# A Mamba cross-attention block with a folded feed-forward: softplus in one ScalarE operation, the dt·u product on VectorE

## The chip, the cores and the metric

The kernel runs on one core of a Trainium2 chip. A core has TensorE (matmuls, into PSUM), VectorE, ScalarE (table-driven functions), GpSimd (which reads and writes SBUF only here) and SyncE, which issues most of the DMAs. Engines run their own instruction streams and wait for each other on semaphores. The metric is the device time of one execution in microseconds (us), the median of several runs.

## What is computed

Four batches, sequence length 512. For each batch a Mamba layer runs over 512 channels with 16 states, gated by the layer-normed input; the result is added to x, then normed again and sent through a sum of eight 512 x 512 factors. The core of the reference:

```python
x = silu(conv1d(hidden @ in_proj.T, conv_w) + conv_b)        # "u"
x_dbl = einsum('bdl,ed->bel', x, x_proj_w)
dt_low, Bm, Cm = split(x_dbl, [16, 32])                       # 16 | 16 | 16 rows
dt = softplus(dt_proj_w @ dt_low + dt_proj_b)                 # (b, 512 channels, 512)
def step(state, inp):                                         # scan over the sequence
    d, b, c, u = inp
    dA = exp(d[..., None] * A)                                # A = -exp(A_log), 16 states
    state = state * dA + (d * u)[..., None] * b[:, None, :]
    return state, einsum('bdn,bn->bd', state, c)
y = (ys + D * x) * silu(layernorm(x_in))
x1 = x_in + y.T
out = x1 + layernorm(x1) @ factors.sum(0) / sqrt(8) + bias
```

## The kernel before

**Tiling.** 128 channels lie on the partitions and the sequence (512) on the free axis. A *step* s = 0..15 handles batch b = s // 4 and channel block k = s % 4. In a step the 16 states go through in eight *pairs* (slots) j = 0..7, each a tile of 128 x 2 x 512. Nothing is scheduled by a planner: each engine's order is written by hand in its function `step(s)`, a loop over j, and semaphore counts tie the engines together.

**What a pair costs each engine.** ScalarE makes two decays, dA = exp(dt * A) (`decay`, L811), into PSUM. There are two such buffers, so ScalarE may write pair j only once VectorE is done with pair j-2 (`decays`, L814 to L823). GpSimd makes h = B * (dt*u) (`times_b`, L1144). VectorE runs the recurrence over the sequence (`scan`, L992) and then multiplies by C (`times_c`, L998); for some pairs the C product is GpSimd's instead (`times_c` of GpSimd, L1137), and then the scan writes to h in SBUF and the PSUM buffer is free as soon as the scan ends. Which pairs these are is set by `on_pool`: j = 0 and 4 in steps 0 to 3, j = 0, 2 and 4 in steps 4 to 14, j = 0 and 2 in step 15. TensorE adds the products into the PSUM bank y with an identity matmul (`state_sum`, L534). h has eight buffers.

**dt for the next step.** During step s the dt of step s+1 is made: TensorE's `dt_proj`, ScalarE's Relu and Abs (`softplus_signs`, after the decays of slot 0), its Exp, Square, Abs and Ln (`softplus_parts`, after slot 1), VectorE's three operations L963, L969 and L975 (`softplus_poly`, `softplus_sum`, in slot 3 for even k and slot 2 for odd k), and GpSimd's product dt*u with the reset of dt's first column (`dt_times_u`, L1130 and L1132, at the end of its step).

**What else sits between the pairs.** VectorE: the gate of the step before (L1006, slot 1), the addition to x (L1034, slot 2 for even k and 3 for odd k), three convolution taps (L949, slots 6, 7 and the next 0) where the convolution isn't TensorE's. ScalarE: in slot 3 of steps with k = 0 the four gates (L705), and in slot 3 of steps 2, 6 and 10 one silu over the next batch's u (L697), each between two table loads, since silu is in another table set than exp and ln; and norms, copies and evacuations of 0.6 to 0.8 us each. TensorE has short filler matmuls (`fill_idle`, L529), 88 of them by the table `IDLE_FILL`.

**The start.** Loads, four input projections, twelve convolution taps on VectorE, four silus, `x_proj`, then the first dt: `first_abs`, `softplus_parts(0)`, the poly and sum on VectorE, dt*u, reset, first decays, first scan. The rows of B and C for a batch go to DRAM and come back spread over the partitions (L340, L346, L351).

Of the kernel before, what the change touches and what calls it, by code (L numbers as in the profile page):

```python
# [31 lines left out]
P = 128  # L32
# [15 lines left out]
RAW_STATS = {8: ((12, 5), (12, 6), (12, 7)), 9: ((13, 2), (13, 2), (13, 3)),  # L48
# [6 lines left out]
POLY_BELOW = 2.0 ** -7  # L55
# [15 lines left out]


def build(nc, x, ctxT, w_inT, channel, x_projT, dt_wT, factors, bias, out):
    bc_dram = nc.dram_tensor("bc_scratch", (BATCH, 2 * N, L), F32, kind="Internal").ap()

    with ExitStack() as ctx:
# [6 lines left out]
        def sem(name):  # L83
# [8 lines left out]
        w_in = sb("w_in", [P, CB, DI])  # L92
# [23 lines left out]
        l_dt = sb("l_dt", [P, L])  # L116
        q_dt = sb("q_dt", [P, L])
# [15 lines left out]
        cols = sb("cols", [P, 4])  # L133
        eps_col, sq_col, below_col, above_col = (cols[:, i:i + 1] for i in range(4))
# [47 lines left out]
        d_mm, d_relu, d_abs, d_exp, d_sq, d_far, d_ln, d_poly, d_log, d_dt, d_dtu = (  # L182
            sem(f"d_{n}") for n in ("mm", "relu", "abs", "exp", "sq", "far", "ln", "poly", "log", "dt", "dtu"))
# [51 lines left out]
        def blocks_at(part, s, at):  # L235

            early = {t: ((t + KB, 5), (t + KB, 6), (t + KB, 7), (t + KB + 1, 0), (t + KB + 1, 4),
# [21 lines left out]
        def on_pool(p):  # L259

            s, j = divmod(p, PAIRS)
            return j in (LAST_POOL_C if s == STEPS - 1 else EARLY_POOL_C if s < KB else POOL_C)

        def sum_order(s):

            return LAST_SUM_ORDER if s == STEPS - 1 else EARLY_SUM_ORDER if s < KB else SUM_ORDER

# [144 lines left out]
        def _(pe):  # L412
            def in_proj(bank, k, first=False):
                for c in range(CB):
# [3 lines left out]
                    mm = pe.matmul(bank[:], w_in[:, c, k * P:(k + 1) * P], ctx_sb[:, c, :],  # L418
# [217 lines left out]
            pe.wait_ge(ctx_landed, 16)  # L636
            in_proj(work0, 0)
# [6 lines left out]
            mm.then_inc(b_first, 1)  # L644
            in_proj(work1, 1)
# [18 lines left out]
        def _(act):  # L664
# [609 lines left out]
```

## Time and profile before

| | |
|---|---|
| median of 3 runs (lowest, highest) | 489.57 us (489.28, 491.35) |
| the profiled execution, its own time | 488.93 us |
| its span | 487.1 us |
| VectorE busy | 467.9 us (96%) |
| GpSimd busy | 448.4 us (92%) |
| TensorE busy (modelled) | 439.7 us (90%) |
| ScalarE busy | 349.7 us (72%) |
| granted TensorE clock, mean | 0.993 |

The views of the profile are: the page's share of busy time by engine; the list of who waited for whom; the timeline, which gives instructions in order of time with the idle time before them; groups of instructions by line and shape; and a table of busy time by stretch. An engine's neighbouring instructions overlap by about 0.1 us in the records, so what one costs is read as the distance from its start to the start of the next.

### The profile page before, as it was taken

The page shows a single profiled execution, that of the slowest core. Times are in us where ns is not written, and L with a number is a line of the kernel's source. Part 1 is how long each engine was busy: PE and PEld are TensorE (multiplying, and loading weights), DVE is VectorE, ACT ScalarE, POOL GpSimd, SP SyncE. Part 2 cuts the span into 40 slices and gives each one's busy share as a digit, 9 for nine tenths or more (in the row PEclk, how much of TensorE's full clock was granted, in tenths as well). Part 3 has the DMA queues.
Part 4 walks back from the last instruction along what each step waited for, and adds up shares of the span by engine and source line. Part 5 has one row for each costly group of instructions (what it writes and reads, how often), then busy time and mean ns, then how long its engine had stood idle before and what let it go on. Part 6 is the DMA issues. An engine that isn't in the chain of part 4 may idle for free.

```text
span 487.1 us, 4317 instructions
## 1 busy us (share of the span) xinstructions
PE 439.7 (90%) x1139; PEld 187.4 (38%) x1154; DVE 467.9 (96%) x366; ACT 349.7 (72%) x625; POOL 448.4 (92%) x235
## 2 busy tenths in 40 slices
PE   8788897999888969999989899889899798998996
PEld 5233343434333333433434343333434343443432
DVE  4899999999999999999999999999999999999996
ACT  2789655978569869797788977698689885743422
POOL 4379899999899999999999999999999999999982
PEclk9999899999999989999999999999999999999999
DMA  6799744439982000100793000000395000000002
GB/s 190 258 361 340 195 81 99 85 70 225 288 341 86 0 0 0 62 5 1 236 412 114 1 22 1 0 22 1 111 393 237 0 23 22 22 22 22 1 0 86
DMA packets 17872, 53.97 MB, mean 111 GB/s; under 512 B 2724, under 2 KB 3236, under 8 KB 16824
## 3 DMA queue, kind: packets, MB, share of 16 engines
q1 hardware_dynamic: 16696, 45.31, 25.8%
q0 software_dynamic: 1152, 8.39, 8.5%
q8 instruction: 9, 0.15, 0.1%
q14 instruction: 15, 0.12, 0.1%
HBM read 49.24 MB, written 4.46 MB: 110 GB/s over the span
## 4 chain that ended last, share of the span: by engine, by line
POOL 61%; issue 18%; DVE 9%; DMA 5%; PE 3%; SPq 2%; ACT 1%; POOLq 0%; DVEq 0%; ACTq 0%
POOL h L1144 40%; POOL h L1137 15%; DVE dA L992 4%; DMA b_rep<-bc_scratch 4%; POOL dtu L1130 3%; DVE acc L949 2%; DVE h L992 1%; POOL fsum L1170 1%; SPq L351 1%; POOL fsum L1174 1%; PE y L534 1%; SPq L346 1%; PE y L624 1%; DVE h L998 1%; POOL x L1188 1%
## 5 line engine op out<-in xcount | busy, mean ns | idle before, releaser
L1144 POOL TENSOR_TENSOR h<-b_rep,dtu 128x1024 f32<-128x1024 f32 x127 | 302.3, 2449 | 13.2 <-DVE dtu L1100 9.8
L534 PE MATMUL y<-h,ident 128*128 128x512 f32 x508 | 240.3, 607 | 30.0 <-DVE h L998 28.9
L811 ACT ACTIVATE dA<-dt,a_neg 128x512 f32<-128x512 f32 x256 | 165.8, 679 | 88.4 <-DVE h L998 76.0
L992 DVE TENSOR_TENSOR_SCAN dA<-dA,h 128x1024 f32<-128x1024 f32 x85 | 194.1, 2283 | 0.5 <-ACT dA L811 0.5
L534 PEld LDWEIGHTS y<-h,ident 128*128 128x128 f32 x508 | 91.9, 191 | 159.1 <-issue 99.9
L1137 POOL TENSOR_TENSOR h<-h,c_rep 128x1024 f32<-128x1024 f32 x43 | 103.4, 2405 | 5.4 <-DVE h L992 5.3
L998 DVE TENSOR_TENSOR h<-dA,c_rep 128x1024 f32<-128x1024 f32 x84 | 102.3, 1218 | 1.4
L992 DVE TENSOR_TENSOR_SCAN h<-dA,h 128x1024 f32<-128x1024 f32 x43 | 98.0, 2279 | 1.4 <-ACT dA L811 1.4
L418 PE MATMUL work<-ctx_sb,w_in 128*128 128x512 f32 x60 | 28.7, 607 | 1.9 <-DVE x L1034 1.4
L522 PE MATMUL work<-fsum,xnT 128*128 128x512 f32 x64 | 28.8, 592 | 0.0
L949 DVE SCALAR_TENSOR_TENSOR acc<-work,chan,acc 128x511 f32<-128x511 f32 (+2 forms) x30 | 21.5, 729 | 5.2 <-ACT acc L670 5.0
L529 PE MATMUL y<-ones,still 128*128 128x512 bf16 x76 | 20.0, 379 | 0.6
L1130 POOL TENSOR_TENSOR dtu<-dt,u 128x512 f32<-128x512 f32 x15 | 19.8, 1318 | 0.0
L430 PE MATMUL work<-row_b,x 128*128 128x512 f32 (+3 forms) x40 | 18.0, 593 | 1.9 <-ACT row_b L678 1.9
L522 PEld LDWEIGHTS work<-fsum,xnT 128*128 128x128 f32 x64 | 12.2, 190 | 15.3 <-issue 15.3
L418 PEld LDWEIGHTS work<-ctx_sb,w_in 128*128 128x128 f32 x60 | 11.2, 194 | 17.2 <-issue 14.9
L565 PE MATMUL y<-u,diag_d 128*128 128x512 f32 x32 | 17.4, 626 | 0.0
L445 PE MATMUL work<-dt_low,w_dt 32*128 32x512 f32 x30 | 16.8, 640 | 0.0
L529 PEld LDWEIGHTS y<-ones,still 128*128 128x128 bf16 x88 | 8.6, 98 | 16.0 <-issue 10.3
L709 ACT ACTIVATE xnT<-x 128x512 f32<-128x512 f32 x13 | 8.1, 620 | 9.0 <-DVE x L1027 9.0
L498 PE MATMUL work<-fsum,x 128*128 128x512 f32 x32 | 14.5, 595 | 0.0
L670 ACT ACTIVATE acc<-work,chan 128x512 f32<-128x512 f32 x10 | 7.7, 766 | 7.3 <-PE work L418 7.3
(141 smaller groups left out, 441.5 us busy)
## 6 DMA issues: line engine op xcount, KB each, us to landing
b_rep<-bc_scratch SPq DMA_DIRECT2D x32, 512.0 KB, 9.2
c_rep<-bc_scratch SPq DMA_DIRECT2D x32, 512.0 KB, 8.8
fsum<-factors POOLq DMA_DIRECT2D x8, 1024.0 KB, 8.1
x<-x SPq DMA_DIRECT2D x4, 1024.0 KB, 7.9
out<-x SPq DMA_DIRECT2D x16, 256.0 KB, 2.0
ctx_sb<-ctxT SPq DMA_DIRECT2D x3, 512.0 KB, 5.7
ctx_sb<-ctxT SPq DMA_DIRECT2D x2, 256.0 KB, 3.6
w_in<-w_inT SPq DMA_DIRECT2D x1, 384.0 KB, 4.3
```

The costliest lines, as they stand in the source:

```text
L418: mm = pe.matmul(bank[:], w_in[:, c, k * P:(k + 1) * P], ctx_sb[:, c, :], start=(c == 0), stop=(c == CB - 1))
L430: mm = pe.matmul(work1[:, i:L], tap_diag[:, k, TAPS - 1 - i, :], x_in[:, 0:L - i], start=(i == 0), stop=(i == TAPS - 1))
L522: pe.matmul(work1[:], xnT[:, k, :], fsum[:, k, :], start=(k == 0), stop=False)
L529: pe.matmul(y[:], still[:], ones[:], start=False, stop=False)
L534: mm = pe.matmul(y[:], ident[:], h[:, (s * PAIRS + j) % H_RING, i, :], start=False, stop=(j == sum_order(s)[-1] and i == 1))
L811: act.activation(dA[:, j % 2, i, :], dt[:, k % 2, :], ACT.Exp, scale=a_neg[:, k, 2 * j + i:2 * j + i + 1]).then_inc(exp_done, 1)
L949: dve.scalar_tensor_tensor(out=acc[:, k, i:L], in0=bank[:, 0:L - i], scalar=cw[:, k, TAPS - 1 - i:TAPS - i], in1=acc[:, k, i:L], op0=ALU.m ...
L992: dve.tensor_tensor_scan(pair if on_pool(s * PAIRS + j) else decay, decay, pair, 0.0, ALU.mult, ALU.add).then_inc(scanned, 1)
L998: dve.tensor_tensor(h[:, (s * PAIRS + j) % H_RING], dA[:, j % 2], c_rep[:, j], ALU.mult).then_inc(mulc, 1)
L1130: pool.tensor_tensor(dtu[:, k % 2, :], dt[:, k % 2, :], u[:, n // KB % 2, k, :], ALU.mult).then_inc(d_dtu, 1)
L1137: pool.tensor_tensor(h[:, p % H_RING], h[:, p % H_RING], c_rep[:, p % PAIRS], ALU.mult).then_inc(pmulc, 1)
L1144: pool.tensor_tensor(h[:, (s * PAIRS + j) % H_RING], b_rep[:, j], dtu[:, k % 2, :].unsqueeze(1).to_broadcast([P, 2, L]), ALU.mult).then_in ...
```

## The change

- **Softplus.** ScalarE's nine-operation share is gone: six ScalarE and three VectorE operations are replaced by one ACTIVATE with the Softplus function, in slot 2 of every step but the last (`SOFTPLUS_SLOT`), between a load of the softplus table set and a load of the exp/ln set. Fifteen such places, and one at the start.
- **dt*u and the reset** move from GpSimd's end of step to VectorE's slot 3, with both inputs (dt, u) in SBUF.
- **C products.** GpSimd has j = 0 and 2 in steps 0 to 3, 5, 6, 13 and 15, and j = 0, 2, 4 in steps 4, 7 to 12 and 14. The order of sums follows.
- **ScalarE's slots.** The four gates and the silu over a batch move from slot 3 to slot 4; a convolution evacuation from slot 2 to 3; g's mean and variance to slot 3 (slot 5 for k = 0).
- **Start.** The first softplus is one operation; two of four statistics, the aggregation and the negation of the first norm move behind the first scan; TensorE makes the first B rows before two input projections; exp(A_log) comes first on ScalarE; the first input weights and the channel table are issued from ScalarE's queue, in layouts that make each partition's part one piece.
- `IDLE_FILL` has 53 filler matmuls.

```diff
+SUM_ORDERS = {(0,): (1, 0, 2, 3, 4, 5, 6, 7), (0, 2): (1, 0, 3, 2, 4, 5, 6, 7), (0, 2, 4): (1, 0, 3, 2, 5, 4, 6, 7),
+              (0, 4): (1, 0, 2, 3, 5, 4, 6, 7)}
+POOL_C = ((0, 2), (0, 2), (0, 2), (0, 2), (0, 2, 4), (0, 2), (0, 2), (0, 2, 4), (0, 2, 4), (0, 2, 4), (0, 2, 4), (0, 2, 4),
+          (0, 2, 4), (0, 2), (0, 2, 4), (0, 2))
+SOFTPLUS_SLOT = 2
...
-            def softplus_signs(n):
+            def softplus(n):
                 act.wait_ge(d_mm, n + 1)
-                if n > 0:
-                    act.wait_ge(d_dt, n)
                 if n >= 2:
                     act.wait_ge(exp_done, (n - 1) * (2 * PAIRS))
                     act.wait_ge(dt_reset, n - 1)
-                act.activation(dt[:, n % 2, :], dt_bank(n)[:], ACT.Relu).then_inc(d_relu, 1)
-                act.wait_ge(d_relu, n)
-                act.activation(dt_bank(n)[:], dt_bank(n)[:], ACT.Abs).then_inc(d_abs, 1)
...
-            def softplus_parts(n):
...
+                act.activation(dt[:, n % 2, :], dt_bank(n)[:], ACT.Softplus).then_inc(d_dt, 1)
...
-                    if j == 0 and is_d:
-                        softplus_signs(s + 1)
-                    if j == 1 and is_d:
-                        softplus_parts(s + 1)
+                    if j == SOFTPLUS_SLOT and is_d:
+                        act.preload_act_table_set("softplus")
+                        softplus(s + 1)
+                        act.preload_act_table_set("natural_log_exp_and_others")
...
-                    if j == 2 and s > 0 and s + KB + 1 in TENSOR_CONV:
+                    if j == 3 and s > 0 and s + KB + 1 in TENSOR_CONV:
                         conv_out(s + KB + 1)
...
-                    if j == 3 and k == KB - 2 and b + 1 < BATCH:
+                    if j == 4 and k == 0:
+                        act.preload_act_table_set("silu_and_others")
+                        gate_batch(b)
+                        act.preload_act_table_set("natural_log_exp_and_others")
+                    if j == 4 and k == KB - 2 and b + 1 < BATCH:
                         act.preload_act_table_set("silu_and_others")
                         silu_batch(b + 1)
                         act.preload_act_table_set("natural_log_exp_and_others")
...
+            def dt_times_u(n):
+                dve.wait_ge(d_dt, n + 1)
+                dve.wait_ge(u_done, n + 1)
+                dve.tensor_tensor(dtu[:, n % 2, :], dt[:, n % 2, :], u[:, n // KB % 2, n % KB, :], ALU.mult).then_inc(d_dtu, 1)
+                dve.wait_ge(d_dtu, n + 1)
+                dve.memset(dt[:, n % 2, 0:1], RESET).then_inc(dt_reset, 1)
...
-                    if j == 3 - k % 2 and is_d:
-                        softplus_poly(s + 1)
-                        softplus_sum(s + 1)
+                    if j == 3 and s + 1 < STEPS:
+                        dt_times_u(s + 1)
...
-                if s + 1 < STEPS:
-                    dt_times_u(s + 1, (k + 1) % KB)
...
-            pe.wait_ge(ctx_landed, 16)
-            in_proj(work0, 0)
             pe.wait_ge(ident_ready, 1)
             pe.wait_ge(bc_evac, 1)
...
             mm.then_inc(b_first, 1)
+            pe.wait_ge(ctx_landed, 16)
+            in_proj(work0, 0)
```

ScalarE's order in step 4 (a step with k = 0), from its slot 1 to the decays after the gates; L811 are the decays, L684 the convolution evacuation. Before:

```order
L811 ACTIVATE dA<-dt,a_neg 128x512 x2
L772 ACTIVATE work<-work 128x512
L774 ACTIVATE q_dt<-work,cols 128x512
L775 ACTIVATE l_dt<-work,cols 128x512
L777 ACTIVATE l_dt<-l_dt,cols 128x512
L811 ACTIVATE dA<-dt,a_neg 128x512 x2
L684 ACTIVATE acc<-work,chan 128x512
L811 ACTIVATE dA<-dt,a_neg 128x512 x2
L899 ACT_TABLE_LOAD
L705 ACTIVATE gate<-x,g_r 128x512 x4
L901 ACT_TABLE_LOAD
L811 ACTIVATE dA<-dt,a_neg 128x512 x2
```

The decays of slots 0 and 1 stood with two and four softplus parts behind them, and the gates came behind the decays of slot 3. Of the change, the same place, where L776 are the decays, L742 the Softplus, L669 the evacuation and L690 the gates:

```order
L776 ACTIVATE dA<-dt,a_neg 128x512 x8
L805 ACT_TABLE_LOAD
L742 ACTIVATE dt<-work 128x512
L807 ACT_TABLE_LOAD
L776 ACTIVATE dA<-dt,a_neg 128x512 x2
L669 ACTIVATE acc<-work,chan 128x512
L776 ACTIVATE dA<-dt,a_neg 128x512 x2
L833 ACT_TABLE_LOAD
L690 ACTIVATE gate<-x,g_r 128x512 x4
L835 ACT_TABLE_LOAD
L776 ACTIVATE dA<-dt,a_neg 128x512 x2
```

Between the decays of slot 2 and slot 3 now stand two table loads and the Softplus, and the gates stand between slots 4 and 5.

VectorE's order in step 4, slots 0 to 5; L992 is the scan, L1006 the gate, L998 the C product, L1034 the addition to x. Before:

```order
L992 SCALAR_TENSOR_TENSOR dA<-dA,h 128x1024
L1006 TENSOR_TENSOR yg<-y,gate 128x512
L998 TENSOR_TENSOR h<-dA,c_rep 128x1024
L992 SCALAR_TENSOR_TENSOR h<-dA,h 128x1024
L1034 TENSOR_TENSOR x<-work,x 128x4x128
L992 SCALAR_TENSOR_TENSOR dA<-dA,h 128x1024
L963 SCALAR_TENSOR_TENSOR work<-q_dt,work 128x512
L969 TENSOR_TENSOR work<-work,l_dt 128x512
L975 TENSOR_TENSOR dt<-work,dt 128x512
L998 TENSOR_TENSOR h<-dA,c_rep 128x1024
L992 SCALAR_TENSOR_TENSOR h<-dA,h 128x1024
L992 SCALAR_TENSOR_TENSOR dA<-dA,h 128x1024
```

Of the change, where L953 is the scan, L967 the gate, L959 the C product, L995 the addition, L941 dt*u and L943 the reset:

```order
L953 SCALAR_TENSOR_TENSOR dA<-dA,h 128x1024
L967 TENSOR_TENSOR yg<-y,gate 128x512
L959 TENSOR_TENSOR h<-dA,c_rep 128x1024
L953 SCALAR_TENSOR_TENSOR h<-dA,h 128x1024
L995 TENSOR_TENSOR x<-work,x 128x4x128
L953 SCALAR_TENSOR_TENSOR dA<-dA,h 128x1024
L941 TENSOR_TENSOR dtu<-dt,u 128x512
L943 MEMSET dt 128x1
L959 TENSOR_TENSOR h<-dA,c_rep 128x1024
L953 SCALAR_TENSOR_TENSOR h<-dA,h 128x1024
L953 SCALAR_TENSOR_TENSOR dA<-dA,h 128x1024
```

In slot 3 the three softplus operations have given way to the product and the one-column reset.

## Rows read from the trace of the kernel before

**Rows 1.** The page's first part: busy time, share, instructions of each engine.

```profile
PE 439.7 (90%) x1139; PEld 187.4 (38%) x1154; DVE 467.9 (96%) x366; ACT 349.7 (72%) x625; POOL 448.4 (92%) x235
```

**Rows 2.** Waits of VectorE: who, for whom, us in total, times, longest.

```profile
DVE h L992 <- ACT dA L811: 1.4, 3, 0.5
...
DVE yg L1006 <- PE y L534: 0.9, 1, 0.9
```

**Rows 3.** Timeline, VectorE, steps 4 and 5: start, duration, engine, line, operation.

```profile
141.79 2.27 DVE L992 TENSOR_TENSOR_SCAN dA<-dA,h 128x1024 f32<-128x1024 f32 x1
...
145.69 2.28 DVE L992 TENSOR_TENSOR_SCAN h<-dA,h 128x1024 f32<-128x1024 f32 x1
147.89 0.67 DVE L1034 TENSOR_TENSOR x<-work,x 128x512 f32<-128x512 f32 x1
148.47 2.29 DVE L992 TENSOR_TENSOR_SCAN dA<-dA,h 128x1024 f32<-128x1024 f32 x1
150.66 0.67 DVE L963 SCALAR_TENSOR_TENSOR work<-q_dt,work 128x512 f32<-128x512 f32 x1
...
152.78 1.21 DVE L998 TENSOR_TENSOR h<-dA,c_rep 128x1024 f32<-128x1024 f32 x1
...
156.21 2.27 DVE L992 TENSOR_TENSOR_SCAN dA<-dA,h 128x1024 f32<-128x1024 f32 x1
158.51 1.22 DVE L998 TENSOR_TENSOR h<-dA,c_rep 128x1024 f32<-128x1024 f32 x1
159.66 2.29 DVE L992 TENSOR_TENSOR_SCAN dA<-dA,h 128x1024 f32<-128x1024 f32 x1
```

**Rows 4.** Timeline, ScalarE: the silu of step 2, then the gates of step 4.

```profile
94.35 1.92 ACT L697 ACTIVATE u<-acc 128x2048 f32<-128x2048 f32 x1
...
145.81 1.30 ACT L811 ACTIVATE dA<-dt,a_neg 128x512 f32<-128x512 f32 x2
147.13 1.28 ACT L899 ACT_TABLE_LOAD   x1
148.42 2.93 ACT L705 ACTIVATE gate<-x,g_r 128x512 f32<-128x512 f32 x4
151.37 1.28 ACT L901 ACT_TABLE_LOAD   x1
```

**Rows 5.** Timeline of the start, all engines; in brackets the idle time before.

```profile
5.91 0.19 PEld L418 LDWEIGHTS work<-ctx_sb,w_in 128*128 128x128 f32 x1 [0.48 <-DMA ctx_sb<-ctxT]
...
19.77 2.47 DVE L954 BATCH_NORM_STATS2 g_stat<-x 128x6 f32<-128x512 f32 x4
...
20.56 0.60 ACT L766 ACTIVATE q_dt<-y 128x512 f32<-128x512 f32 x1 [0.93 <-PE y L445]
...
22.15 0.36 DVE L958 BATCH_NORM_AGGREGATE g_mv<-g_stat 128x2 f32<-128x6 f32 x4
...
22.37 1.98 PE L642 MATMUL dA<-dt_low,ident 64*128 64x512 f32 x4
...
25.53 0.69 DVE L1100 TENSOR_TENSOR dtu<-dt,u 128x512 f32<-128x512 f32 x1
...
26.29 0.06 DVE L1102 MEMSET dt<- 128x1 f32 x1
...
27.80 2.29 DVE L992 TENSOR_TENSOR_SCAN h<-dA,h 128x1024 f32<-128x1024 f32 x1 [0.31 <-ACT dA L811]
```

**Rows 6.** Groups by line and shape: count, busy us, mean ns, idle before.

```profile
L1144 POOL TENSOR_TENSOR h<-b_rep,dtu 128x1024 f32<-128x1024 f32 x127 | 302.3, 2449 | 13.2 <-DVE dtu L1100 9.8 <-issue 2.2 <-DMA b_rep<-bc_scratch 0.9
L1137 POOL TENSOR_TENSOR h<-h,c_rep 128x1024 f32<-128x1024 f32 x43 | 103.4, 2405 | 5.4 <-DVE h L992 5.3
...
L1130 POOL TENSOR_TENSOR dtu<-dt,u 128x512 f32<-128x512 f32 x15 | 19.8, 1318 | 0.0
...
L759 ACT ACTIVATE dt<-work 128x512 f32<-128x512 f32 x15 | 8.7, 580 | 2.0 <-PE work L445 1.9
```

**Rows 7.** Busy by stretch: length, PE, PEld, DVE, ACT, POOL, granted clock, DMA.

```profile
170.00:174.00 4.00, 0.56 (x3) 0.59 (x4) 4.00 (x4) 3.36 (x7) 4.00 (x3) 0.89 0.00 0
174.00:178.00 4.00, 4.00 (x10) 1.84 (x9) 3.90 (x4) 3.39 (x7) 4.00 (x4) 0.68 0.00 0
```

More of the change, by code:

```diff
@@ L132, in build @@
         t_r = sb("t_r", [P, 3, KB])
-        cols = sb("cols", [P, 4])
-        eps_col, sq_col, below_col, above_col = (cols[:, i:i + 1] for i in range(4))
+        eps_col = sb("eps_col", [P, 1])[:]
         dA = ps("dA", [P, 2, 2, L])
@@ L181, in build @@
         c_landed = [sem(f"c_landed{j}") for j in range(PAIRS)]
-        d_mm, d_relu, d_abs, d_exp, d_sq, d_far, d_ln, d_poly, d_log, d_dt, d_dtu = (
-            sem(f"d_{n}") for n in ("mm", "relu", "abs", "exp", "sq", "far", "ln", "poly", "log", "dt", "dtu"))
+        d_mm, d_dt, d_dtu = (sem(f"d_{n}") for n in ("mm", "dt", "dtu"))
         y_init = sem("y_init")
@@ L235, in blocks_at @@
         def blocks_at(part, s, at):
-            early = {t: ((t + KB, 5), (t + KB, 6), (t + KB, 7), (t + KB + 1, 0), (t + KB + 1, 4),
+            early = {t: ((t + KB, 5), (t + KB, 6), (t + KB, 7), (t + KB + 1, 1), (t + KB + 1, 4),
                          (t + KB + 2, -1), (t + KB + 2, 2)) for t in range(2 * KB)}
@@ L417, in in_proj @@
                         pe.wait_ge(w_in_first, 16)
-                    mm = pe.matmul(bank[:], w_in[:, c, k * P:(k + 1) * P], ctx_sb[:, c, :],
+                    mm = pe.matmul(bank[:], w_in[:, k, c, :], ctx_sb[:, c, :],
                                    start=(c == 0), stop=(c == CB - 1))
@@ L853, in step @@
                         conv_out(KB + 1)
-                    if j == 2 and s > 0 and s + KB + 1 in TENSOR_CONV:
+                    if j == 3 and s > 0 and s + KB + 1 in TENSOR_CONV:
                         conv_out(s + KB + 1)
-                    if j == (4 if k == 0 and s > 0 else 2) and is_g:
+                    if j == (5 if k == 0 else 3) and is_g:
                         act.wait_ge(x_landed, (b + 2) * 16)
@@ L865, in step @@
                         act.preload_act_table_set("natural_log_exp_and_others")
-                    if j == (5 if k == 0 and s > 0 else 4 - k % 2) and is_g:
+                    if j == (5 if k == 0 else 3) and is_g:
                         var_sum(g_mv, b + 1, k, g_scratch, g_mean, s + 1, g_var)
@@ L916, in _ @@
                 first_silu(k)
+            act.preload_act_table_set("softplus")
+            x_evac(0)
+            softplus(0)
             act.preload_act_table_set("natural_log_exp_and_others")
-            x_evac(0)
-            act.activation(a_neg[:], a_log, ACT.Exp).then_inc(a_exp, 1)
-            first_abs()
-            softplus_parts(0)
-            conv_tap(work0, KB)
-            lnv(g_r, g_mv, slice(0, KB), g_aggr, KB, g_lnv)
-            expv(g_r, slice(0, KB), g_lnv, 1, g_expv)
-            act.wait_ge(g_neg, 1)
+            act.wait_ge(bc_evac, 1)
+            act.wait_ge(dtl_evac, 1)
             act.wait_ge(a_ready, 1)
@@ L1039, in step @@
                 nv = s + KB + 2
-                is_c, is_d = nv < STEPS and nv not in TENSOR_CONV, s + 1 < STEPS
+                is_c = nv < STEPS and nv not in TENSOR_CONV
                 for j in range(PAIRS):
                     scan(s, j)
+                    if s == 0 and j == 0:
+                        for i in range(2, KB):
+                            stats(g_stat, 0, i, g_bn)
+                        for i in range(KB):
+                            aggr(g_mv, g_stat, i, g_bn, i + 1, g_aggr)
+                        dve.wait_ge(g_aggr, KB)
+                        dve.tensor_scalar(g_mv[:, :, 0], g_mv[:, :, 0], -1.0, None, ALU.mult).then_inc(g_neg, 1)
                     if s == 0 and j in (0, 1):
```

108 lines of the change are left out of this document (26 added, 82 removed).

## The prediction, made before the changed kernel had run

> **What bounds the kernel now.** I read the shares of busy time first: VectorE is busy 96% of the span, GpSimd 92%, TensorE 90% by a modelled figure, ScalarE 72% [rows 1]. Shares say nothing of who waits, so the list of waits comes next. Once the steps run, VectorE waits for ScalarE 1.9 us in total (0.3 of it ahead of the first scan) and for TensorE once, 0.9 us, and in no row of that list for GpSimd [rows 2, 5]. GpSimd has waited for VectorE's scans, 5.3 us [rows 6]. So VectorE sets the end from the first scan at 27.80 us on, GpSimd is close behind it, and the question for each edit is what it does to VectorE's stream, and then whether VectorE begins to wait.
>
> The timeline gives the price of each piece of that stream, start to start [rows 3]. A pair whose C product is VectorE's takes 3.45 us (156.21 to 159.66), a pair whose product is GpSimd's 2.20 us (145.69 to 147.89). An operation of half the width between them adds 0.58 us (147.89 to 148.47), the gate 0.45 (141.79 to 145.69 is 3.90).
>
> **The softplus leaves VectorE.** With its three operations, scan to C product takes 4.31 us (148.47 to 152.78), without them 2.30 (156.21 to 158.51): 2.0 us, fifteen times, 30.2 us, all on the bounding engine. In their place come dt*u and the reset. The only such pair of VectorE in the trace is at the start: 0.76 us from the product's start to the reset's (25.53 to 26.29) [rows 5], so scan to C product becomes 2.19 + 0.76 + 0.03 = 2.98, which is 0.68 more than 2.30; fifteen times 10.2 us. Net **-20.0 us**, if dt*u costs in the steps what it cost at the start, where GpSimd stood idle. In the steps GpSimd is nearly always in a product of 2.45 us that reads SBUF [rows 6], and VectorE's operations there take at least one input from PSUM, whereas dt*u takes both from SBUF. No row shows such an operation beside GpSimd's. Its price is bounded below by no wait and above by one whole GpSimd product, 2.45 us a time. The nearest rows, scans and C products beside GpSimd's, keep 2.27 to 2.29 and 1.21 to 1.22 us [rows 3], so I take no wait; the other end is the first rival.
>
> **GpSimd** loses fifteen times 1.32 us and the reset, and three C products of 2.41 us (steps 5, 6, 13) [rows 6], some 28 us of 448. It does not bind afterwards. VectorE takes the three products back: 3 x (3.45 - 2.20) = **+3.8 us**. In steps 0 to 3 slot 2 takes the place of slot 4, at no cost.
>
> **ScalarE** is where part of the gain goes. Its decays for pair j may start only when pair j-2 has left PSUM, so it can't work ahead through a long insertion. A table load and what follows start 1.29 us apart (147.13, 148.42), the four gates take 2.95, the silu over a batch 1.92, and a pair of decays 1.30, 1.32 ahead of a load [rows 4]; Softplus I price as the Relu it replaces, same shape and banks, 0.58 [rows 6]. Take step 4 and count from the start of scan 1. VectorE: scan 2 at 3.90, scan 3 at 6.7 (2.20 and the addition, 0.58), scan 4 at 6.7 + 2.98 + 1.15 = 10.8, and, its product being GpSimd's, scan 5 at 13.0. ScalarE: decays of slot 2 from 0.1, load, Softplus, load to 4.6, decays of slot 3 to 5.9, an evacuation of 0.6 to 6.5, decays of slot 4 to 7.8, load, gates, load to 13.4, decays of slot 5 to 14.7. So Softplus itself is hidden (slot 3's decays are done 0.8 us early; where there is no addition 0.2 us), but scan 5 waits 1.7 us. Before, the same gates stood behind slot 3 and were covered exactly by the three operations that now go. The same working for the other places, with the small operations of 0.6 to 0.7 us that stand there: 1.9 us in step 2 (silu 1.92 in place of gates, but more small work ahead of it), 0.7 in step 6, 1.8 in step 8, 1.9 in step 10, 2.3 in step 12, 0.75 in step 0, 0.4 in step 11, and 0.4 in step 0 for the first B rows: 11.9 us, of which 1.6 are there already [rows 2]. Net **+10.3 us**.
>
> The Trainium skill speaks against this edit: its page ScalarE: Activation LUTs, section What ACT_TABLE_LOAD costs, gives about 2.66 us for every switch of sets, the load and a drain. The trace disagrees: a load is 1.28 us and the gates start 1.29 us after it [rows 4]. By the page each Softplus run would be 2.8 us longer and scan 3 would wait some 2.3 us in fifteen steps, which alone would eat the gain.
>
> **The start.** Before, the Abs began at 20.56, right behind dt's matmul, and the first scan at 27.80 [rows 5]. Now Softplus runs 20.56 to 21.16, dt*u and the reset end by 22.0, the load ends at 22.5, the decays at 23.8. TensorE's first B rows, 1.98 us from 22.37, start two input projections earlier, at 20.4, so the first product (1.22 us) is also done at 23.7. First scan at 23.85, 3.95 us earlier. The second half of the context is issued one DMA earlier, and TensorE waited 0.48 us for it: 0.45 more, bounds 0 and 0.5. But two of four statistics (half of 2.47 us), the aggregations (0.36) and a negation (put at 0.2) now stand behind the first scan, on the bounding engine: +1.8. Net **-2.6 us**.
>
> **TensorE.** The fillers that go add nothing to the sum; its one late sum (0.9 us) comes after work that doesn't change and stays.
>
> **Sum:** -20.0 + 3.8 + 10.3 - 2.6 = -8.5 us. The profiled execution took 488.9 us, 0.6 under the median: 480.4, or **481.0** as a median.
>
> **Rival 1: dt*u waits for GpSimd.** If the two engines exclude each other, VectorE waits for the end of the running product. At a random moment that is 0.92 x 2.45 / 2 = 1.1 us. In the seven steps that wait for ScalarE anyway (0, 2, 4, 6, 8, 10, 12) it is nearly covered, all but 0.4 us in each of steps 0 and 6; in the other eight it is not: 9.8 us, and the time is **490.8**. It decides from a mean wait of 1.0 us on (no gain left), and makes the kernel slower by 0.5% from about 1.25 us on; with the longest wait it would be 502. Against it: nothing in the trace, since none of VectorE's operations in the steps has two SBUF tensors. The skill's page SBUF — State Buffer, section Who interferes with whom, states this rule: a VectorE instruction with both inputs in SBUF contends with a GpSimd instruction that reads SBUF, and the loser blocks for the whole instruction. No row here shows it; by that rule the time is this rival's. Chance 0.33, of which 0.11 slower by over 0.5%, 0.14 within, 0.08 faster (waits that fall well).
>
> **Rival 2: TensorE's clock.** In step 5 TensorE was busy 0.56 us of four and then ran four microseconds at a granted 0.68 of full speed, between its levels of 1.2 and 2.4 GHz [rows 7]. The new waits of VectorE in slot 5 make such holes in six steps and 35 fillers are gone. Each dip costs TensorE up to 2 us; it has about 2.5 us of room before the next gate, save in step 12, which is late already. Up to 3 us: **484**. Chance 0.10 (0.02 of it within 0.5%).
>
> **Rival 3: the switches or Softplus cost more than rows 4 and 6 say**, or Softplus is not one operation. Each 0.5 us over the 0.2 us of room in slots 2 and 3 costs some 6 us: with 1 us more, **493**, and slower. Nothing speaks for it but that no row shows the third set. Chance 0.08.
>
> **Numbers.** Forecast 481.0, chance 0.49. Measurement can tell about 0.5% (2.4 us). Faster by more: 0.49 + 0.08 + 0.08 = 0.65; within: 0.14 + 0.02 = 0.16; slower: 0.11 + 0.08 = 0.19. The forecast's own range is 476.5 (ScalarE's waits half of what I count) to 484; to hold 8 in 10 it must reach through the first rival's middle: 476.5 to 492.5.
>
> **What would show it.** First scan near 23.4 us. Scan to C product in slot 3 near 3.0 us: near 4 instead, or a dt*u record longer than 0.7 us, is rival 1. VectorE waits for ScalarE of 1.5 to 2.3 us ahead of scan 5 in steps 2, 4, 8, 10 and 12 and none ahead of scan 3. Fifteen loads of 1.28 us with Softplus 1.3 us behind. GpSimd waiting for scans some 20 us in total. A TensorE wait at a gate beyond 0.9 us is rival 2.

## The result, and the profile after

| | before | after |
|---|---|---|
| median of runs | 490.15 us (489.28 to 491.35, 4 runs) | 530.22 us (525.4 to 534.37, 4 runs) |
| ratio after / before | | 1.078, 95% interval 1.069 to 1.088 |
| profiled execution, its span | 488.9, 487.1 us | 534.37, 532.5 us |

The changed kernel is 8% slower: 40 us, where 8.5 us less were forecast, and far outside the range of 476.5 to 492.5. The profiled execution of after is its slowest, 4 us over the median, and the ratio is taken without it (the two medians alone give 1.082).

The shares of busy time, to be set against [rows 1]:

```profile
PE 458.3 (86%) x1119; PEld 194.4 (37%) x1119; DVE 505.0 (95%) x348; ACT 345.1 (65%) x578; POOL 424.6 (80%) x202
```

VectorE has 18 instructions fewer and is busy 37 us longer (505.0 against 467.9). GpSimd went down by 24 us, near the 28 that were worked out from [rows 6]. So the time came into VectorE's own instructions, and the groups (line, engine, operation, shape, count, busy us, mean ns, idle before) say into which:

```profile
L953 DVE TENSOR_TENSOR_SCAN dA<-dA,h 128x1024 f32<-128x1024 f32 x88 | 201.0, 2284 | 8.1 <-ACT dA L776 7.4
...
L959 DVE TENSOR_TENSOR h<-dA,c_rep 128x1024 f32<-128x1024 f32 x87 | 106.2, 1220 | 1.5
...
L941 DVE TENSOR_TENSOR dtu<-dt,u 128x512 f32<-128x512 f32 x16 | 62.3, 3893 | 0.7 <-ACT dt L742 0.7
```

Scans and C products cost per piece what they cost before [rows 3]. The sixteen dt*u take 62.3 us. The first, at the start, takes 0.69; sixteen of that kind would be 11.0, so 51.3 us are too many. They do not stand in the profile as idle time: they lie inside the records of the dt*u themselves. Whoever reads the list of waits alone, as in [rows 2] (now for ScalarE 7.4 and 1.3 us, for TensorE 3.1, for GpSimd 0.6), doesn't find them. Seven of the sixteen, from the timeline of VectorE (start, duration): the first three, three short ones and the last:

```profile
21.40 0.69 DVE L941 TENSOR_TENSOR dtu<-dt,u 128x512 f32<-128x512 f32 x1 [0.71 <-ACT dt L742]
...
39.92 2.85 DVE L941 TENSOR_TENSOR dtu<-dt,u 128x512 f32<-128x512 f32 x1
...
68.35 11.27 DVE L941 TENSOR_TENSOR dtu<-dt,u 128x512 f32<-128x512 f32 x1
...
171.53 1.17 DVE L941 TENSOR_TENSOR dtu<-dt,u 128x512 f32<-128x512 f32 x1
...
200.41 0.68 DVE L941 TENSOR_TENSOR dtu<-dt,u 128x512 f32<-128x512 f32 x1
...
322.74 1.14 DVE L941 TENSOR_TENSOR dtu<-dt,u 128x512 f32<-128x512 f32 x1
...
472.23 8.07 DVE L941 TENSOR_TENSOR dtu<-dt,u 128x512 f32<-128x512 f32 x1
```

The longest, 68.35 to 79.62, with GpSimd's timeline beside it:

```profile
66.38 2.60 POOL L1091 TENSOR_TENSOR h<-b_rep,dtu 128x1024 f32<-128x1024 f32 x1
68.70 1.11 POOL L1117 DMA_DIRECT2D fsum<-factors  x1
69.31 2.88 POOL L1091 TENSOR_TENSOR h<-b_rep,dtu 128x1024 f32<-128x1024 f32 x1
71.62 2.87 POOL L1084 TENSOR_TENSOR h<-h,c_rep 128x1024 f32<-128x1024 f32 x1
73.91 5.15 POOL L1091 TENSOR_TENSOR h<-b_rep,dtu 128x1024 f32<-128x1024 f32 x2
79.70 2.38 POOL L1091 TENSOR_TENSOR h<-b_rep,dtu 128x1024 f32<-128x1024 f32 x1 [0.64 <-DVE dtu L941]
```

GpSimd goes from product to product (each record begins before the one ahead of it ends) up to 79.06. Then its next product needs the very dt*u that VectorE holds, GpSimd stands still, and 0.56 us later dt*u is done: about the 0.69 that it takes alone. VectorE did not wait for one product but for the end of the queue. The record at 105.20 reads the same way: GpSimd's products run to 111.88, dt*u ends at 112.43. The fifteen dt*u of the steps fall into two kinds. Seven end only when GpSimd stands still, two to five products on, and hold 42.5 of the 51.3 us. The other eight wait for the running product at most, though GpSimd goes on without a pause in seven of them (between the products of the eighth, at 39.92, stands a DMA issue). The one at 171.53 ends at 172.70, 0.56 us behind the product that ran (to 172.14):

```profile
169.79 2.35 POOL L1084 TENSOR_TENSOR h<-h,c_rep 128x1024 f32<-128x1024 f32 x1
172.11 5.16 POOL L1091 TENSOR_TENSOR h<-b_rep,dtu 128x1024 f32<-128x1024 f32 x2
```

GpSimd's next pair of products is 5.16 us long here, against 4.70 for the pair at 262.11, which let nothing through. So a queue without a pause can hold VectorE to its end, but does not do so every time, and nothing in the trace tells the places apart.

That is a reading of one trace, and it comes after the fact. The experiments test it.

### The profile page after: what moved, and what is told of

It reads as the page before. It is cut to its first block, busy times and chain, and to the rows that moved or that the text cites. A ratio compares the mean times of both kernels' runs of the same rounds, so it can differ in the third digit from the quotient of the medians.

```text
span 532.5 us, 4118 instructions
## 1 busy us (share of the span) xinstructions
PE 458.3 (86%) x1119; PEld 194.4 (37%) x1119; DVE 505.0 (95%) x348; ACT 345.1 (65%) x578; POOL 424.6 (80%) x202
## 4 chain that ended last, share of the span: by engine, by line
DVE 52%; issue 18%; PE 18%; ACT 7%; DMA 2%; POOL 1%; DVEq 0%; SPq 0%; ACTq 0%; POOLq 0%
DVE dA L953 25%; DVE dtu L941 11%; PE y L519 10%; DVE h L953 7%; DVE h L959 5%; ACT dA L776 3%; DVE acc L920 2%; PE work L423 2%; PE work L507 2%; DMA b_rep<-bc_scratch 1%; POOL h L1091 1%; DVE x L995 1%; ACT gate L690 1%; DMA bc_scratch<-dt_low 1%; PE y L609 1%
## 5 line engine op out<-in xcount | busy, mean ns | idle before, releaser
L1091 POOL TENSOR_TENSOR h<-b_rep,dtu 128x1024 f32<-128x1024 f32 x127 | 305.4, 2445 | 41.2 <-PE y L519 22.6
L519 PE MATMUL y<-h,ident 128*128 128x512 f32 x508 | 259.4, 655 | 61.0 <-DVE h L959 58.0
L776 ACT ACTIVATE dA<-dt,a_neg 128x512 f32<-128x512 f32 x256 | 165.9, 680 | 125.7 <-DVE h L959 109.0
L953 DVE TENSOR_TENSOR_SCAN dA<-dA,h 128x1024 f32<-128x1024 f32 x88 | 201.0, 2284 | 8.1 <-ACT dA L776 7.4
L519 PEld LDWEIGHTS y<-h,ident 128*128 128x128 f32 x508 | 100.4, 206 | 203.3 <-issue 117.7
L1084 POOL TENSOR_TENSOR h<-h,c_rep 128x1024 f32<-128x1024 f32 x40 | 96.4, 2411 | 38.0 <-DVE h L953 38.0
L959 DVE TENSOR_TENSOR h<-dA,c_rep 128x1024 f32<-128x1024 f32 x87 | 106.2, 1220 | 1.5
L953 DVE TENSOR_TENSOR_SCAN h<-dA,h 128x1024 f32<-128x1024 f32 x40 | 91.2, 2279 | 1.5 <-ACT dA L776 1.3
L941 DVE TENSOR_TENSOR dtu<-dt,u 128x512 f32<-128x512 f32 x16 | 62.3, 3893 | 0.7 <-ACT dt L742 0.7
L430 PE MATMUL work<-dt_low,w_dt 32*128 32x512 f32 x30 | 19.7, 739 | 0.0
L514 PE MATMUL y<-ones,still 128*128 128x512 bf16 x53 | 14.0, 381 | 0.0
```

Source lines behind the costliest of these rows:

```text
L430: pe.matmul(dt_bank(n)[:], w_dt[0:BC_ROW, n % KB * P:(n % KB + 1) * P], dt_low[0:BC_ROW, :], start=True, stop=True).then_inc(d_mm, 1)
L519: mm = pe.matmul(y[:], ident[:], h[:, (s * PAIRS + j) % H_RING, i, :], start=False, stop=(j == sum_order(s)[-1] and i == 1))
L776: act.activation(dA[:, j % 2, i, :], dt[:, k % 2, :], ACT.Exp, scale=a_neg[:, k, 2 * j + i:2 * j + i + 1]).then_inc(exp_done, 1)
L941: dve.tensor_tensor(dtu[:, n % 2, :], dt[:, n % 2, :], u[:, n // KB % 2, n % KB, :], ALU.mult).then_inc(d_dtu, 1)
L953: dve.tensor_tensor_scan(pair if on_pool(s * PAIRS + j) else decay, decay, pair, 0.0, ALU.mult, ALU.add).then_inc(scanned, 1)
L959: dve.tensor_tensor(h[:, (s * PAIRS + j) % H_RING], dA[:, j % 2], c_rep[:, j], ALU.mult).then_inc(mulc, 1)
```

## The experiments

Theory A: an operation of VectorE with both inputs in SBUF doesn't run while GpSimd's products, which read SBUF, follow each other back to back. The rivals: it waits for the running product only; dt*u is slow for another reason (what it writes, the DMA traffic); the loss lies in TensorE's clock, or in Softplus and its tables. In each diff "-" is the kernel that the edit starts from. Each is given with its ratio to the kernel before on the same chip (median 490.75 us beside experiments 1 to 4, 489.5 to 489.6 beside the others).

**1. dt*u reads PSUM.** Everything else stands where the change put it, save that TensorE's waits before it refills the bank now go by dt*u (left out below).

```diff
                 act.activation(dt[:, n % 2, :], dt_bank(n)[:], ACT.Softplus).then_inc(d_dt, 1)
+                if n > 0:
+                    act.wait_ge(d_dt, n + 1)
+                    act.activation(dt_bank(n)[:], dt_bank(n)[:], ACT.Softplus).then_inc(d_copy, 1)
...
-                dve.tensor_tensor(dtu[:, n % 2, :], dt[:, n % 2, :], u[:, n // KB % 2, n % KB, :], ALU.mult).then_inc(d_dtu, 1)
+                if n > 0:
+                    dve.wait_ge(d_copy, n)
+                dve.tensor_tensor(dtu[:, n % 2, :], dt[:, 0, :] if n == 0 else dt_bank(n)[:], u[:, n // KB % 2, n % KB, :], ALU.mult).then_inc(d_dtu, 1)
```

> The changed kernel, but in steps 1 to 15 ScalarE also writes the softplus in place into its PSUM bank (a second Softplus, 0.60 us), and VectorE's dt*u reads dt from that bank instead of SBUF; TensorE may refill the bank only after dt*u. Nothing else differs. Theory A (an operation of VectorE with both inputs in SBUF doesn't start while GpSimd runs product behind product; one input in PSUM frees it): every dt*u about 0.7 us instead of a mean of 3.89, so the 51 us go, 530 - 51 = 479, and the second Softplus delays slot 3's decays by up to 0.4 us in the steps without an addition: 478 to 486. Theory B (dt*u is slow for what it writes, or for DMA traffic, or the loss is TensorE's clock or the table loads): dt*u stays near 3.9 us and the time near 530, or a few us above it for the second Softplus.

Measured: 489.42 us (10 runs), ratio to before 0.9985, interval 0.996 to 1.001. The same place as above, VectorE and then GpSimd:

```profile
65.58 2.27 DVE L958 TENSOR_TENSOR_SCAN dA<-dA,h 128x1024 f32<-128x1024 f32 x1
67.77 0.67 DVE L946 TENSOR_TENSOR dtu<-work,u 128x512 f32<-128x512 f32 x1
```
```profile
66.12 2.48 POOL L1096 TENSOR_TENSOR h<-b_rep,dtu 128x1024 f32<-128x1024 f32 x1
68.45 0.97 POOL L1122 DMA_DIRECT2D fsum<-factors  x1
69.06 2.75 POOL L1096 TENSOR_TENSOR h<-b_rep,dtu 128x1024 f32<-128x1024 f32 x1
71.44 2.67 POOL L1089 TENSOR_TENSOR h<-h,c_rep 128x1024 f32<-128x1024 f32 x1
```

GpSimd's queue is the same, piece by piece; dt*u takes 0.67 us in place of 11.27. The group of all fifteen:

```profile
L946 DVE TENSOR_TENSOR dtu<-work,u 128x512 f32<-128x512 f32 x15 | 10.1, 672 | 0.0
```

It writes the same SBUF tile, beside the same transfers and products, so the inputs decide, and theory A holds against the rest. The 40 us are back, in one edit that leaves the slots, the tables and the fillers alone. Neither TensorE's clock (granted 0.986 here, 0.922 in the profile of after, with the same fillers) nor the table loads were the cause. The time is 3.4 us above the range given; what holds it there is taken up below.

**2. dt*u on GpSimd again**, as in the kernel before; the rest of the change stays. (The function moves to GpSimd's part too; left out below.)

```diff
-                    if j == 3 and s + 1 < STEPS:
-                        dt_times_u(s + 1)
...
+                if s + 1 < STEPS:
+                    dt_times_u(s + 1, (k + 1) % KB)
```

> The changed kernel, but dt*u and the reset of steps 1 to 15 are GpSimd's again, at the end of its step, as in the kernel before. Theory A: VectorE loses 16 x 3.9 us and more comes back than the 51 us, since also the 0.7 us each goes: 530 - 51 - 10 = 469; GpSimd gets 15 x 1.32 = 20 us more on its 425 and stays below VectorE's load (505 - 62 = 443), but close to it, so it may bind: 469 to 480. Theory B (the loss lies in TensorE's clock, in table loads and Softplus, or in the slots): the loss stays whatever engine makes dt*u, so 520 or more.

Measured: 483.93 us (4 runs), ratio 0.9855, interval 0.983 to 0.988: faster than before by 1.4%; with experiment 7's, which is the same within the noise, the fastest version here. The loss is gone with the operation, as theory A has it, but it is 4 us above the range. VectorE is busy 11 us less than in experiment 1 (443.2 against 454.2) and gets half of that:

```profile
DVE dA L953 <- ACT dA L776: 17.0, 13, 2.6
DVE yg L967 <- PE y L519: 3.5, 1, 3.5
...
DVE h L953 <- POOL h L1096: 1.4, 1, 1.4
```

(waits of VectorE: for whom, us in total, times, longest). Experiment 1 has 13.8 in the first row. A faster VectorE covers less of ScalarE's insertions.

**3. That move alone, in the kernel before.**

```diff
                         softplus_sum(s + 1)
+                        dve.wait_ge(d_dt, s + 2)
+                        dve.wait_ge(u_done, s + 2)
+                        dve.tensor_tensor(dtu[:, (s + 1) % 2, :], dt[:, (s + 1) % 2, :], u[:, (s + 1) // KB % 2, (s + 1) % KB, :],
+                                          ALU.mult).then_inc(d_dtu, 1)
+                        dve.wait_ge(d_dtu, s + 2)
+                        dve.memset(dt[:, (s + 1) % 2, 0:1], RESET).then_inc(dt_reset, 1)
...
-                if s + 1 < STEPS:
-                    dt_times_u(s + 1, (k + 1) % KB)
```

> The kernel before, with one part of the change alone: dt*u and the reset of steps 1 to 15 on VectorE, right behind its softplus operations, instead of on GpSimd. Theory A: VectorE's dt*u has to wait for a pause in GpSimd's products, which are at 92% of the span there and gain 20 us of room: 15 x 0.7 us plus waits like those of the changed kernel (a mean excess of 3.2 us): 490 + 10 + 48 = 548, range 520 to 560. The price that the prediction took (no wait) gives 490 + 10 = 500; one GpSimd product at most each time (mean 1.1 us) gives 517.

Measured: 564.12 us (4 runs), ratio 1.146, interval 1.140 to 1.153. One step of VectorE's timeline:

```profile
201.27 0.69 DVE L975 TENSOR_TENSOR dt<-work,dt 128x512 f32<-128x512 f32 x1
202.00 9.36 DVE L1059 TENSOR_TENSOR dtu<-dt,u 128x512 f32<-128x512 f32 x1
```

Two operations of the same engine, kind and width follow each other; the first has one input in PSUM (work), the second none. Fifteen dt*u take 67.1 us, 56.8 over 0.69 each. The profiled execution took 568.6 us, 79.7 more than that of the kernel before: this excess and the added 10 us are 67 of them, new waits of VectorE another 7.4 (for ScalarE's decays 7.5 us in place of 1.9, for TensorE's sums 2.7 in place of 0.9), and 5 us stay unexplained. The median is 4 us above the range. Of the change's parts this one alone is worse than all together: no Softplus, no table, no C split is needed for the loss.

**4. A pause in GpSimd's queue.** No work is added; GpSimd waits for something.

```diff
+                    if j == 6 and s + 1 < STEPS:
+                        pool.wait_ge(d_dtu, s + 2)
                     if p > 0:
                         times_b(b, s, k, j)
```

> The changed kernel with one wait more: GpSimd doesn't begin its B product of slot 6 until dt*u of the next step is done. No work is added or moved. Theory A: GpSimd stands still at about the time that VectorE comes to dt*u, so each waits at most for the product under way: dt*u at most 3.1 us, mean near 1.2, some 40 of the 51 us come back: 480 to 497. If instead dt*u is slow for what it reads and writes, or by DMA traffic, the wait brings nothing, since it only takes time from GpSimd: 530 or more. If the long dt*u records are waits for one product each, a pause in the queue behind that product changes nothing either: 530.

Measured: 499.63 us (4 runs), ratio 1.017, interval 1.014 to 1.020: 31 us faster than the changed kernel, by a wait, though 2.6 us above the range. The sixteen dt*u take 31.4 us in place of 62.3. Some are still long, and they show why. VectorE, then GpSimd:

```profile
67.81 6.88 DVE L941 TENSOR_TENSOR dtu<-dt,u 128x512 f32<-128x512 f32 x1
```
```profile
66.18 2.46 POOL L1091 TENSOR_TENSOR h<-b_rep,dtu 128x1024 f32<-128x1024 f32 x1
68.51 0.96 POOL L1117 DMA_DIRECT2D fsum<-factors  x1
69.12 2.73 POOL L1091 TENSOR_TENSOR h<-b_rep,dtu 128x1024 f32<-128x1024 f32 x1
71.48 2.65 POOL L1084 TENSOR_TENSOR h<-h,c_rep 128x1024 f32<-128x1024 f32 x1
74.78 4.75 POOL L1091 TENSOR_TENSOR h<-b_rep,dtu 128x1024 f32<-128x1024 f32 x2 [0.64 <-DVE dtu L941]
```

Here GpSimd still had three products ahead of the new wait (slots 4 and 5 and a C product). VectorE sat through all of them, until the last ended at 74.13, and was done 0.56 us after. I had put the longest at 3.1; that was wrong, as I had taken it that GpSimd stands at the wait by then.

**5. GpSimd drains between two products.** In every slot it waits for its own last product before it starts the next. (The helper, which waits for the count of its own products, is left out below.)

```diff
                     if p > 0:
+                        own_products_done(p)
                         times_b(b, s, k, j)
                     if p >= C_LAG and on_pool(p - C_LAG):
+                        pool.wait_ge(mulb, p + 1)
                         times_c(p - C_LAG)
```

> The changed kernel, but GpSimd waits for its own previous product to be complete before it starts the next one, in every slot. Same work, same order, dt*u of VectorE in the same place; GpSimd's products are no longer issued back to back, but with a drained pipe and a semaphore between two of them (some 0.1 us each, 170 products: 17 us more on an engine that is 80% busy). Theory A1 (the lock passes to VectorE as soon as one product of GpSimd has ended with nothing issued behind it): no dt*u record above 2.45 + 0.67 = 3.1 us, mean about 1.7, the mean excess 1.0 in place of 3.2, so 530 - 35 = 495, range 488 to 505. Theory A2 (it needs a pause longer than a semaphore wait, as where GpSimd waits for another engine): records of 5 us and more stay and the time is 525 or more. Theory B (dt*u is slow for another reason) gives the same 525 or more, and is already spoken against by the version that reads dt from PSUM.

Measured: 492.57 us (10 runs), ratio 1.005, interval 1.003 to 1.007. By the medians 38 of the 40 us are back, by some 170 waits on the engine that VectorE was blocked by. VectorE, then GpSimd, at the same place:

```profile
67.36 2.10 DVE L941 TENSOR_TENSOR dtu<-dt,u 128x512 f32<-128x512 f32 x1
```
```profile
66.51 2.40 POOL L1091 TENSOR_TENSOR h<-b_rep,dtu 128x1024 f32<-128x1024 f32 x1
68.86 0.80 POOL L1117 DMA_DIRECT2D fsum<-factors  x1
69.47 2.57 POOL L1091 TENSOR_TENSOR h<-b_rep,dtu 128x1024 f32<-128x1024 f32 x1
```

dt*u ends at 69.46, 0.55 us behind the product that ran when it came (to 68.91), and GpSimd's next product starts at 69.47. No dt*u is longer than 2.76, and the group's mean is 1.62:

```profile
L941 DVE TENSOR_TENSOR dtu<-dt,u 128x512 f32<-128x512 f32 x16 | 25.9, 1621 | 0.9 <-ACT dt L742 0.9
```

This separates the two forms of theory A: one drained moment between products is enough. What costs is that products without such a moment let VectorE in at some boundaries (eight of fifteen in after) and hold it to the end of the run at others.

**6. The price of the drain by itself:** experiment 1's version with the same waits.

> The version in which VectorE's dt*u reads PSUM (489.4), with GpSimd's wait for its own previous product in every slot: the price of these waits by themselves, where there is nothing of VectorE's to let through. GpSimd is 87% busy there; 170 waits of 0.1 us are 17 us, which just fit: 489 to 494. What this version is above 489.4 is what the waits cost in the changed kernel too; what that one (492.6) is above this one is what is left of VectorE's waits for single products, 15 x 0.9 = 14 us less the second Softplus: about 5.

Measured: 491.07 us (9 runs), ratio 1.003, interval 1.0015 to 1.0046: against experiment 1 the waits cost 1.6 us by the medians, 2.2 by the ratios. Experiment 5 is only 1.1 (ratios) to 1.5 us above this one, though its dt*u are 14.9 us longer than sixteen of 0.69. VectorE waited 5.7 us for ScalarE's decays there against 14.3 here, so more than half of the blocked time, by this reading, lies where VectorE would have waited for ScalarE anyway. The expectation had 5 us for this difference: about four too many.

**7. The fillers of the kernel before**, in experiment 2's version (88 in place of 53; the expectation counts one too many in each):

```diff
-IDLE_FILL = {(0, -1): 14, (0, 3): 3, (1, 3): 4, (3, 3): 4, (4, 1): 3, (5, 6): 2, (7, 6): 2, (8, 1): 2, (8, 6): 2, (9, 6): 2,
-             (10, 1): 4, (11, 1): 2, (12, 1): 3, (13, 1): 3, (14, 3): 3}
+IDLE_FILL = {(0, -1): 14, (0, 3): 3, (0, 6): 3, (1, 3): 6, (2, 3): 3, (3, 3): 6, (4, 1): 5, (5, 6): 3, (6, 1): 2,
+             (7, 6): 4, (8, 1): 3, (8, 3): 2, (8, 6): 4, (9, 6): 4, (10, 1): 6, (11, 1): 3, (11, 6): 2, (12, 1): 5,
+             (13, 1): 5, (14, 3): 5}
```

> The version with dt*u on GpSimd (483.9), with the idle fillers of TensorE as in the kernel before (89 in place of 54). VectorE waited 3.5 us there for TensorE's sum at the gate of step 13, where the kernel before has 0.9. If the thinner fillers cost TensorE its clock, that wait goes back to 0.9 and the granted clock rises: 481. If it comes from the late work of step 12 alone, the time stays at 484 or rises a little for the 35 fillers.

Measured: 483.59 us (4 runs), ratio 0.989, interval 0.984 to 0.994, against 483.93 and 0.9855 without; granted clock 0.975 in both, the late sum of step 13 3.7 us in place of 3.5. The fillers change nothing here. The wait at that gate has another cause; the late work of step 12, the expectation's other branch, was not tested by itself.

**8 and 9. The gates elsewhere.** Experiment 2's version with ScalarE's four gates behind slot 6 in place of slot 4 (8), and at the end of slot 6, behind the convolution tap (9):

```diff
-                    if j == 4 and k == 0:
+                    if j == 6 and k == 0:
                         act.preload_act_table_set("silu_and_others")
                         gate_batch(b)
```

> The version with dt*u on GpSimd (483.9), and ScalarE's four gates of a batch, with their two table loads, behind slot 6 instead of slot 4. In slot 4 VectorE's two pairs that cover them take 3.45 + 2.20 us, in slot 6 3.45 + 3.45 and a convolution part where there is one; the insertion is the same 5.5 us. So the waits of 2.2, 2.0 to 2.4 and 2.6 us ahead of scan 5 in steps 4, 8 and 12 should go down to about 1 us each, and step 0's too: 4 to 5 us: 479 to 480.5. If those waits are made by something else than the gates' place (Softplus and its two loads), no change: 483.9.

> The version with dt*u on GpSimd (483.9), with the four gates at the end of slot 6, behind the first convolution tap or copy of that slot. With the gates ahead of it the tap came 3.85 and 4.48 us late in steps 4 and 8. Insertion and tap need 5.5 + 0.6 us and two pairs of decays 2.6, VectorE's pairs 5 and 6 give 6.9 + 0.7: a wait of about 1.1 us in each of steps 0, 4, 8 and 12 instead of 2.2 to 2.6: 4 to 5 us less: 479.5. If the tap in front makes the decays of slot 7 late by as much as was won, 484.

Measured: 485.15 us (4 runs) and 485.4 us (6 runs), ratios 0.9907 and 0.9904 (intervals 0.988 to 0.993): not faster than the 0.9855 of experiment 2, rather 1 to 2.5 us slower. The gain of 4 to 5 us came in neither; in 9 the expectation's other branch did. The waits of VectorE in 8, and in 9:

```profile
DVE dA L953 <- ACT dA L776: 10.6, 9, 2.4
DVE acc L920 <- ACT acc L655: 10.1, 3, 4.5
```
```profile
DVE dA L953 <- ACT dA L776: 19.6, 12, 3.9
```

In 8 the decays' wait falls by 6.4 us and the tap's rises by 8.9; in 9 the tap is in time and the decays of slot 7 are late, by 3.31 us in step 4 where I had worked out 1.1. The insertion with its two loads finds no cover in either place: the wait moves, it does not go.

## Why the prediction was wrong

**The step that failed is the price of dt*u**, in the second part: "bounded below by no wait and above by one whole GpSimd product, 2.45 us a time". The upper bound was wrong. Fifteen times the mean excess of 3.4 us (51.3 / 15) is what the trace of after has, and single ones took 11.27, 8.07 and 7.23. Even the bound as I put it, all fifteen at one whole product, gave 502; the measured 530 lies 28 above. (By the text's own terms it should have been some 507: 2.45 us in eight steps, and in the other seven 17.2 less the 11.1 that their waits for ScalarE cover.) The error has two layers. First the value: between the ends I took "no wait", since the nearest rows, scans and C products beside GpSimd's, kept their times [rows 3]. But each of those has an input in PSUM, and that difference, which the text itself names, is the one that decides (experiment 1: 0.672 us with PSUM, 3.89 without). A row is near only in what matters for the question. Then the bound: "VectorE waits for the end of the running product" supposes that the other engine lets go between any two products. It did in eight of the fifteen places; in the other seven GpSimd's products, issued back to back, left no such moment until GpSimd stood still.

**Rival 1** had the mechanism. The Trainium skill's page SBUF — State Buffer, section Who interferes with whom, states it, and experiments 1 and 3 agree. But it says that the loser blocks for the whole instruction; here the loser blocked for up to five instructions, and never for more than one where a wait stood between them (experiment 5). The rival's price of a single wait holds where its premise does: with the queue drained the excess is 14.9 us in fifteen, 1.0 each against the 1.1 that I worked out. Its total does not: 492.6 less some 2 for the waits is 490.6, near my 490.8, but that is luck. The waits raised the time by 1.1 to 1.5 us over experiment 6's version, which carries a second Softplus, and not by 9.8, and the sum that they were added to was 8.4 us too low. Its chance of 0.33, of which 0.11 to "slower", was too small, and with waits of this length nearly all of it belonged to "slower".

**The sum without that term** can be checked on experiment 1, where dt*u costs what I put: 489.4 against 481.0, with its own second Softplus (0.6 us, fifteen times on ScalarE). So 8.4 us of the forecast gain were missing besides. By parts, experiment 1's trace against my terms:

- *The start.* First scan at 24.21 us (after: 24.02); 23.85 less 0.45 for the context, 23.4, was summed: 0.6 to 0.8 late. VectorE stands 0.46 us between the reset and the first B rows.
- *Statistics in step 0.* The negation, put at 0.2 us, took 1.87 (1.73 in after). Its only tensor lies in SBUF, and it now stands beside GpSimd's first products; in experiment 2 it came as a product ended and took 0.17. Its record in after ends at 29.53, GpSimd's product at 29.50, and then GpSimd paused: the same cause as dt*u, by this reading, in a place where I hadn't looked: +1.7. But the four aggregations just ahead of it also read and write SBUF alone, ran beside the same product, and took the 0.36 us that they took before [rows 5]; so a tensor in SBUF is not enough for an operation with one input, and what sets the negation apart no run tells. GpSimd and VectorE in after:

```profile
27.13 2.37 POOL L1091 TENSOR_TENSOR h<-b_rep,dtu 128x1024 f32<-128x1024 f32 x1 [10.88 <-DMA b_rep<-bc_scratch]
...
27.40 0.36 DVE L929 BATCH_NORM_AGGREGATE g_mv<-g_stat 128x2 f32<-128x6 f32 x4
27.80 1.73 DVE L1011 TENSOR_SCALAR g_mv<-g_mv 128x4 f32<-128x4 f32 x1
```

- *ScalarE's waits.* I had 11.9 us, ahead of scan 5 in the even steps above all. Experiment 1 has 13.8 in twelve, the longest 2.6. In experiment 2's timeline of step 4, where I had worked out 1.7:

```profile
149.86 1.28 ACT L835 ACT_TABLE_LOAD   x1
151.16 1.30 ACT L776 ACTIVATE dA<-dt,a_neg 128x512 f32<-128x512 f32 x2
```
```profile
148.00 2.28 DVE L953 TENSOR_TENSOR_SCAN h<-dA,h 128x1024 f32<-128x1024 f32 x1
152.49 2.30 DVE L953 TENSOR_TENSOR_SCAN dA<-dA,h 128x1024 f32<-128x1024 f32 x1 [2.21 <-ACT dA L776]
```

  Right in place and mechanism, a little small: +1.9. In after itself they are 8.7 us (7.4 and 1.3), since a blocked VectorE leaves ScalarE time.
- *TensorE and GpSimd.* The late sum took 2.4 us in place of 0.9, and VectorE waited 1.4 us for B products in the first two steps, where I had only 0.4: +2.5.
- Those are some 7 of the 8.4 us; the rest, and how much of the first three is the second Softplus's, isn't separated.

**Softplus and its tables** cost what was forecast. After, ScalarE's timeline in slot 2 of step 0:

```profile
31.62 1.28 ACT L805 ACT_TABLE_LOAD   x1
32.92 0.60 ACT L742 ACTIVATE dt<-work 128x512 f32<-128x512 f32 x1
33.53 1.28 ACT L807 ACT_TABLE_LOAD   x1
34.97 1.30 ACT L776 ACTIVATE dA<-dt,a_neg 128x512 f32<-128x512 f32 x2 [0.15 <-DVE h L959]
```

1.28 a load, Softplus 1.30 behind it and 0.60 long (0.58 was put). Rival 3 is out. The 2.66 us a switch of the Trainium skill's page ScalarE: Activation LUTs, section What ACT_TABLE_LOAD costs, do not show in this trace either: start to start it is 1.30.

**Rival 2** is out as a cause: the fillers change nothing (experiment 7). The clock did fall in after; as experiment 1 has the same fillers and no such fall, I take it for a consequence. Busy time by stretch in after, in the columns of [rows 7], while dt*u was blocked and just behind it:

```profile
68.40:79.60 11.20, 2.79 (x7) 0.95 (x5) 11.20 (x2) 1.21 (x3) 10.66 (x6) 0.76 0.63 140
79.60:82.60 3.00, 1.59 (x2) 0.84 (x3) 2.93 (x4) 1.30 (x2) 2.90 (x2) 0.50 0.00 0
```

TensorE had 2.79 us of work in 11.2 and ran the next sums at 0.50, the lower level (1.2 GHz). Experiment 1 has 1.00 in the 3 us from 79.0 on.

**The rest of the change** was worth making: with dt*u left on GpSimd it gives 483.9, 1.4% less than before. How much of that is Softplus and how much the new start, no run separates. Of the 30.2 us that leave VectorE most is still not seen in the time: ScalarE's waits are 17.0 us where 1.9 were, TensorE's 3.5, GpSimd's 2.4, and three C products came over at 3.8.

## What to carry to other kernels

Before work goes from GpSimd to VectorE, look where its inputs lie. An operation of VectorE with both inputs in SBUF, beside a GpSimd that issues product behind product, can be held for the length of that queue and not only for one instruction. Give it one input in PSUM, leave it on GpSimd, or let GpSimd drain between its products (some 2 us for 170 waits here). And where no row of a trace shows a pair of things side by side, "the nearest rows show no effect" is no ground for zero if those rows differ in exactly the property in question.

## What the runs showed of the hardware

- A VectorE multiplication of 128x512 from SBUF and SBUF took 0.67 to 11.27 us beside GpSimd's products, and 0.67 to 0.68 in all fifteen steps with one of its inputs in PSUM (experiment 1).
- When it was held, it ended 0.55 or 0.56 us behind the end of a product: in after the fifth (79.06 to 79.62) or the first (172.14 to 172.70), with a wait in GpSimd's queue the third (74.13 to 74.69), with the queue drained the first (68.91 to 69.46).
- Products of GpSimd without a pause between them let it in after one at most in seven of the fifteen places of after (in an eighth a DMA issue stood between them) and held it for two to five in the other seven. What decides, no run here tells.
- A DMA issue between two products of GpSimd does not always let it through: in after dt*u got in at the one at 42.13 (dt*u from 39.92 to 42.77, the next product from 42.78), and not at the one at 68.70.
- With GpSimd's wait for its own product it got through every time, at the latest at the end of the product that ran (at most 2.76 us, experiment 5).
- The trace books the blocked time as busy time of the blocked instruction: VectorE stood at 95% with 51 us of nothing in it.
